# A decoder layer on one core: the inputs centred by ScalarE in place of the weights, the bias row spread by PE, loads split and reordered, new engine orders

## The reference

```python
x = x + attn(layernorm(x), Wqkv, bqkv, Wo, bo)      # 16 heads of 8, softmax over 64 positions
x = x + xattn(layernorm(x), ctx, ctx, wq, wk, wv, wo)   # autocorrelation: FFT along each row of 64, top 4 lags
x = x + ffn(layernorm(x), gate_w, w_up, w_down, expert_bias)

def layernorm(x): return (x - mean(x)) / sqrt(var(x) + 1e-5)     # no gain, no bias

def ffn(x, ...):                                     # 8 experts of 256 hidden units
    scores = sigmoid(x @ gate_w.T)
    sel = top_k(scores + expert_bias, 2)
    for e in range(8):
        w_t = sum(where(sel == e, scores[sel], 0))
        h = square(relu((x * w_t) @ w_up[e].T))
        out += h @ w_down[e].T
```

## Time and profile before

| | |
|---|---|
| median of 3 runs | 128.04 us (127.9 to 128.95) |
| time of the profiled execution | 128.05 us |
| its span | 126.3 us |
| PE busy | 112.8 us (89%) |
| DVE busy | 86.4 us (68%) |
| ACT busy | 76.6 us (61%) |
| POOL busy | 45.7 us (36%) |
| mean granted TensorE clock | 0.986 |

### The profile page before, as it was taken

One profiled execution on the slowest core, in us unless ns is written; L12 is line 12 of the kernel. 1 busy time (PEld: TensorE's weight loads), 2 busy tenths in 40 slices (PEclk: granted clock), 3 DMA queues, 4 the chain that ended last, 5 costly groups with the idle time before them and its releaser, 6 DMA issues.

```text
span 126.3 us, 4128 instructions
## 1 busy us (share of the span) xinstructions
PE 112.8 (89%) x1588; PEld 100.1 (79%) x1588; DVE 86.4 (68%) x332; ACT 76.6 (61%) x175; POOL 45.7 (36%) x81
## 2 busy tenths in 40 slices
PE   0269999979998798699999999999999999999990
PEld 0035777769875667578999999999999999999990
DVE  0224999977999457999649598927878736750671
ACT  0510549777957176937899542987914967477840
POOL 8714429525509503495633015401520040510000
PEclk9999999999999769999999999999999999999999
DMA  4899800000000000000000000100001000010001
GB/s 94 240 341 381 340 5 0 0 8 5 0 8 5 5 0 0 5 3 0 5 0 0 3 5 0 47 0 0 3 5 44 0 0 5 0 42 0 0 5 42
DMA packets 4531, 5.20 MB, mean 41 GB/s; under 512 B 288, under 2 KB 3744, under 8 KB 4384
## 3 DMA queue, kind: packets, MB, share of 16 engines
q1 hardware_dynamic: 3792, 3.87, 9.3%
q10 hardware_dynamic: 720, 1.07, 3.1%
HBM read 4.41 MB, written 0.52 MB: 39 GB/s over the span
## 4 chain that ended last, share of the span: by engine, by line
PE 83%; DVE 6%; DMA 4%; issue 3%; ACT 1%; SPq 0%; DVEq 0%
PE ps L807 23%; PE ps L796 19%; PE ps L660 6%; PE ps L689 5%; PE ps L699 5%; DMA wa_sb<-w_cen 4%; PE ps L756 3%; PE ps L646 3%; PE ps L715 2%; PE ps L670 2%; PE ps L747 1%; PE ps L639 1%; PE ps L765 1%; PE ps L739 1%; PE ps L679 1%
## 5 line engine op out<-in xcount | busy, mean ns | idle before, releaser
L807 PE MATMUL ps<-wdn_sb,hid 128*128 128x128 f32 x256 | 31.6, 276 | 0.0
L612 DVE SCALAR_TENSOR_TENSOR x<-ps,w,x 128x128 f32<-128x128 f32 x64 | 19.1, 343 | 16.7 <-PE ps L807 16.5
L807 PEld LDWEIGHTS ps<-wdn_sb,hid 128*128 128x128 f32 x256 | 29.9, 192 | 0.2
L433 ACT ACTIVATE hid<-rel 128x512 f32<-128x512 f32 x32 | 19.6, 629 | 5.9 <-PE ps L807 5.7
L427 ACT ACTIVATE rel<-ps 128x512 f32<-128x512 f32 x32 | 17.8, 595 | 7.2 <-PE ps L796 6.8
L298 POOL TENSOR_TENSOR praw<-praw,negm 128x512 f32<-128x512 f32 x16 | 16.6, 1056 | 13.4 <-DVE negm L502 13.4
L796 PE MATMUL ps<-xhi,whi 128*128 128x256 f32 x64 | 18.5, 289 | 0.0
L796 PE MATMUL ps<-xhi,wlo 128*128 128x256 f32 x64 | 18.0, 282 | 0.0
L796 PE MATMUL ps<-xlo,whi 128*128 128x256 f32 x64 | 18.0, 281 | 0.0
L286 POOL TENSOR_SCALAR rstd<-mv 128x2 f32<-128x2 f32 x12 | 2.6, 218 | 34.4 <-DVE mv L466 34.3
L796 PEld LDWEIGHTS ps<-xhi,whi 128*128 128x128 f32 x64 | 12.0, 188 | 0.4 <-POOL xlo L319 0.2
(11 more groups left out here) (102 smaller groups left out, 195.6 us busy)
## 6 DMA issues: line engine op xcount, KB each, us to landing
wup_sb<-w_up SPq DMA_DIRECT2D x2, 512.0 KB, 7.5
wdn_sb<-w_down SPq DMA_DIRECT2D x1, 1024.0 KB, 9.7
x_sb<-x SPq DMA_DIRECT2D x4, 128.0 KB, 7.0
c_sb<-ctxt SPq DMA_DIRECT2D x1, 512.0 KB, 8.4
out<-x SPq DMA_DIRECT2D x4, 128.0 KB, 1.8
con<-consts ACTq DMA_DIRECT2D x1, 328.0 KB, 5.9
row_sb<-rows ACTq DMA_DIRECT2D x1, 260.0 KB, 5.2
wmid_sb<-w_mid ACTq DMA_DIRECT2D x1, 256.0 KB, 6.7
```

The source lines that it names most:

```text
L433: nc.scalar.activation(hid[:, u % 3, :], rel[:, u % 3, :], ACT.Square).then_inc(done["sq"], 1)
L612: nc.vector.scalar_tensor_tensor(x12[:, 2 * a + t, :], psum("down", a, e)[:, D * t:D * (t + 1)], w2[:, a, t, e:e + 1], x12[:, 2 * a + t, : ...
L807: last = mm(y_ps[:, D * t:D * (t + 1)], hid[:, u % 3, 2 * P * half + P * t:2 * P * half + P * (t + 1)], wdn_sb[:, e, half, :], start=(half ...
```

## The change

The mean is now taken off the rows. `xc` and `x3c` (ACT) compute mean - x with the mean as a bias and a scale of -1, before the transposes `xt` and `xt3`, which read the new buffers. All that follows has the other sign, which is set right where results are used: `nat` and `x1` subtract, the bias row is subtracted, `eg` uses rstd in place of its negative (so POOL's `nrstd` falls away), `rel` has a scale of -1. Steps `wu`, `wc` of the qkv and gate weights and the first `wce` are gone; a `wc` of 128 columns for the query weights stays. `whi` (ACT) and `wlo` (now POOL) read the up weights from SBUF.

The bias row arrives on one partition; `rb` (PE), a product of a row of ones with it, spreads it over 128 partitions, and `rbe` (ACT) copies it. The expert bias has a small load of its own. The context is loaded by chunk, the constants and the middle weights in parts, and x in chunk 1 through ACT. All four orders are rewritten.

```diff
-C_ID, C_CEN, C_POW = 0, 128, 256
+C_ID, C_POW = 0, 128
...
-xt.0.0@0 wc.0.0@1 qkv.0.0@2 qkv.0.1@3 xt.1.0@4 wc.1.0@5 cdft.0.0@6 qkv.1.0@7 qkv.1.1@0 xt.2.0@1 cdft.1.0@2 qkv.2.0@4
+rb.0.0@0 xt.0.0@1 qkv.0.0@2 qkv.0.1@3 wc.0.0@4 xt.1.0@5 cdft.0.0@6 qkv.1.0@7 qkv.1.1@1 cproj.0.0@0 xt.2.0@2 xt.3.0@4
...
-zero.0.0 rs1.0.0 rs1.1.0 xb.0.0 rs1.2.0 psub.0.0 psub.0.1 psub.0.2 psub.0.3 rs1.3.0 psub.1.0 psub.1.1 psub.1.2 psub.1.3
+zero.0.0 zv.0.0 rs1.0.0 rs1.1.0 rs1.2.0 xb.0.0 rs1.3.0 wlo.0.0 wlo.0.1 psub.0.0 psub.0.1 psub.0.2 psub.0.3 wlo.0.2 psub.1.0
...
             sp.dma_start(wa_sb[:, 0:A_Q], w_cen[:, 0:A_Q]).then_inc(ld_qkv, 16)
-            sp.dma_start(x_sb[:, 2:4, :], xv[:, 2:4, :]).then_inc(ld_x[1], 16)
-            sp.dma_start(c_sb[:], cv).then_inc(ld_c, 16)
-            sp.dma_start(x_sb[:, 4:6, :], xv[:, 4:6, :]).then_inc(ld_x[2], 16)
-            sp.dma_start(x_sb[:, 6:8, :], xv[:, 6:8, :]).then_inc(ld_x[3], 16)
+            x_chunk(2)
+            c_chunk(0)
+            c_chunk(1)
+            x_chunk(3)
+            c_chunk(2)
+            c_chunk(3)
...
+                if name == "wlo":
+                    two = slice(2 * part, 2 * part + 2)
+                    pool.wait_ge(done["whi"], NTH[("whi", 0, part)])
+                    nc.gpsimd.tensor_tensor(wlo[:, two].rearrange("p e h -> p (e h)"), wup_sb[:, two].rearrange("p e h -> p (e h)"),
+                                            whi[:, two].rearrange("p e h -> p (e h)").bitcast(F32), ALU.subtract).then_inc(done["wlo"], 1)
...
-            act.dma_start(row_sb[:], rows.partition_broadcast(P)).then_inc(ld_row, 16)
-            act.dma_start(con[:, C_FWD:C_LEN], consts[:, C_FWD:C_LEN]).then_inc(ld_con, 16)
+            act.dma_start(x_sb[:, 2:4, :], x.rearrange("(t p) d -> p t d", p=P)[:, 2:4, :]).then_inc(ld_x[1], 16)
+            act.dma_start(row1[:], rows.unsqueeze(0)).then_inc(ld_row, 16)
+            act.dma_start(con[:, C_FWD:C_INV], consts[:, C_FWD:C_INV]).then_inc(ld_fwd, 16)
+            act.dma_start(wmid_sb[:, 0:W_O2], w_mid[:, 0:W_O2]).then_inc(ld_mid, 16)
             act.dma_start(wa_sb[:, A_Q:A_LEN], w_cen[:, A_Q:A_LEN]).then_inc(ld_wa, 16)
-            act.dma_start(wmid_sb[:], w_mid).then_inc(ld_mid, 16)
+            act.dma_start(wmid_sb[:, W_O2:W_LEN], w_mid[:, W_O2:W_LEN]).then_inc(ld_o, 16)
+            act.dma_start(con[:, C_INV:C_LEN], consts[:, C_INV:C_LEN]).then_inc(ld_con, 16)
+            act.dma_start(eb_sb[:], ebias.partition_broadcast(P)).then_inc(ld_eb, 16)
...
+                if name == "xc":
+                    act.wait_ge(done["st1"], NTH[("st1", a, 0)])
+                    if a >= 2:
+                        act.wait_ge(full["xt"], NTH[("xt", a - 2, 0)])
+                    for t in range(2):
+                        last = nc.scalar.activation(xc[:, a % 2, t, :], x_sb[:, 2 * a + t, :], ACT.Identity, bias=mv[:, a, t, 0:1],
+                                                    scale=-1.0)
+                    last.then_inc(done["xc"], 1)
...
-                if name == "wlo":
-                    dve.wait_ge(done["whi"], NTH[("whi", 0, part)])
...
+                if name == "rb":
+                    pe.wait_ge(ld_row, 16)
+                    mm(bank(name, 0), row1[:, R_ONE:R_LEN], row1[:, 0:R_ONE], start=True, stop=True).then_inc(full[name], 1)
```

203 lines of the change are left out of this document (106 added, 97 removed).

## The result

In 20 runs of each kernel on one chip the median went from 127.81 to **127.69 us** (125.79 to 129.50); the forecast was 124.0. The ratio is 0.9888, with a 95% interval of 0.9854 to 0.9922: faster by 1.1%, where 3.2% had been forecast. By the medians of all runs the gain is 0.1%. The profiled execution took 126.66 us with a span of 123.0, and its clock was whole (mean granted clock 0.998).

A forecast was written before the change was run, and what follows sets the result against it. PE and DVE were each close to being the bound up to 59.9 us, then PE ran without a gap. 128.05 - 0.8 (start) - 3.44 (`wu`) + 0.2 (chunk 2) = 124.0 us, own bounds 123.3 to 125.0, range 120.3 to 126.6.

The forecast's parts named there:

- The start: Up to `qkv.0`: it starts at 8.2 instead of 8.95 over ACT's path; 0.8 us gained, bounds 1.5 gained, 2.5 lost.
- the gain of 0.8 survives: Front, after `qkv.0`: ACT is tight, yet `qkv.1` starts at about 12.3 instead of 13.2, keeping the start's 0.8 us.
- The same pace had been priced only as a bound: First PE products: `qkv.0` stays at its slow pace; the pace rising earlier is the bound of 1.5 us gained.
- The four `wu` products: PE, centring of the up weights: four 128x512 products go, 3.44 us, all on the chain.
- PE's sum, 57.8: First `up`: by PE's work, 59.89 - 0.8 - 3.44 + 2.2 = 57.8 us, the start time chosen.
- DVE's 58.5: First `up`: with DVE's idle time as before, 59.89 - 0.8 - 2.05 + 1.5 = 58.5 us.
- the slow stretch of before: PE, 42.5 to 46.5 us: mostly at 1.2 GHz instead of 2.4, costing 1.7 us, 3.05 with the gap.
- DVE's chain decides: Rival, chance 0.15: DVE sets the first `up`, `x2.0` standing behind `pvt.3` and `val.3`; 125.7 us.
- The 1.0 us that it had for waiting on chunk 3's softmax: Before `x2.0`: DVE waits about 1 us for chunk 3's softmax if POOL is a step behind; part of a 0.15 rival.
- D: Experiments' theory, up to the first `up`: DVE's queue decides its start, so time off PE isn't on the path.
- the gap and the slow clock don't come back: Rival, chance 0.27: PE's 1.35 us gap and the slow clock's 1.7 us vanish with the new order; 121.0 us.
- The experts' stretch: From the first `up`: PE's 63.5 us loses 2.2 us moved ahead and stays gapless; 0.2 us added for chunk 2.

The follow-up runs named there:

- e1: Kernel before without the four products that centre the up weights, centring of the experts' input left out: median 127.71 us, ratio 0.9971.
- e12: Kernel after with the four up-weight centring products put back on PE, results not read: median 127.12 us, ratio 0.9911.
- a0: Kernel after, unaltered, measured a second time: median 127.57 us, ratio 0.9838 to the kernel before.
- e6: e2 with chunk 3's four `psub` on POOL replaced by a one-column memset: median 123.65 us, ratio 0.9636 to the kernel before.
- e10: e11 with DVE's `top.0` and `hit.0` moved clear of `psub`: median 124.30 us, ratio 0.9597 to the kernel before.
- e4: Kernel after with the four `wlo` steps back on DVE: median 129.09 us, ratio 1.0121 to the kernel before.
- e13: e10 with the four up-weight centring products put back on PE, results not read: median 128.04 us, ratio 1.0004 to the kernel before.
- e3: Kernel after with ACT's last three loads issued by SP behind the up weights: median 124.73 us, ratio 0.9712 to the kernel before.
- e2: Kernel after with PE's `pv.1` moved behind three steps, away from `score.3`: median 126.30 us, ratio 0.9782 to the kernel before.
- e5: e2 with 26 unread transposes of the unit matrix put where PE waits: median 125.28 us, ratio 0.9774 to the kernel before.
- e8: Kernel after with `pv.1` and `dft.0` ahead of `score.3` on PE: median 125.06 us, ratio 0.9758 to the kernel before.
- e11: Kernel after with e2's order and e3's loads together: median 124.55 us, ratio 0.9705 to the kernel before.
- e9: e1 with `wlo` moved to POOL, in the old orders: median 127.51 us, ratio 0.9957 to the kernel before.

## Why the prediction was wrong

**The start** was forecast rightly up to `qkv.0`. The table load began at 5.09 (5.0 forecast), `xc.0` and `xt.0` took 0.69 and 0.66, `qkv.0` began at 8.44 (8.2). Its gain of 0.8 us measured 0.5. But "the gain of 0.8 survives" failed: `qkv.1` came at 13.45, not 12.3, and in the chain before it had come at 13.20. The slow pace of the first products lasted until about 13.3, as it had until 13 before, so none of the start's gain was left at `qkv.1`. The same pace had been priced only as a bound. The prediction calls it PE's clock; the windows give a granted clock of 1.00 there in both kernels, so the pace is measured and its cause isn't.

**The four `wu` products** are the step that failed. The sum took "3.44 us, all on the chain" off the time in full. The chain of waits had named them rightly, but the same chain ran over DVE from 48.45 to 57.0, between the last of them and the first `up`, where the prediction read PE "nearly everywhere". The earlier trace rows had shown PE 3.9 us and DVE 6.5 us short of full over 46.7 us, so a gain of 3.44 on PE had to come out of DVE's waits. The median without them in the kernel before is that of before (e1, ratio 0.9971), and the median with them back is that of the changed kernel (e12, 0.9911). In both comparisons the kernel with less work on PE spent more time at half clock, and only a part of the 3.44 us showed at equal clock or at the first up, 1.07 in e1's profile (with 1.6 us more on DVE) and 0.9 to 2.2 in e12. The text said that "taking work off one alone buys little" and then chose PE's sum, 57.8, over DVE's 58.5 for the first up. It came at 59.04, 1.24 us later, and this in an execution without a slow stretch. The forecast had kept the slow stretch of before in its sum; with one, in a0, the first up came at 60.49, 2.7 us late, and later than before the change (59.89).

**DVE's chain decides**, a rival with 0.15, is nearest to what happened, by another route and not in full. The 1.0 us that it had for waiting on chunk 3's softmax was not seen as such; `x2.0` runs right behind `val.3` at 54.80. Beyond that stand three long steps beside `psub`, 1.90 us together, of which e6 shows 1.4 to 1.75 and e10 1.2 us to be on the path. The prediction had read the two lengths of `val` in the earlier trace rows and quoted the rule for it, from the Trainium skill, page "SBUF — State Buffer", section "Who interferes with whom": a DVE instruction with two inputs in SBUF and a GpSimd instruction that reads SBUF shut each other out. It dismissed it because most of DVE's long instructions have one input. The rule holds in this trace: `dif` and `hit` have two, and take 0.86 and 1.15 us beside `psub` where they take 0.17 and 0.29 alone. It is the short instructions with two inputs that pay, and the order should have been looked through for them. What speaks against D alone: 3.4 us more on DVE cost 1.5 us (e4), 3.44 us more on PE reached the first up with 0.86 (e12) and 2.3 (e13), and the front with 1.16 (e3). Both engines are close to being the bound, as the prediction's first paragraph has it.

**The slow clock.** The rival "the gap and the slow clock don't come back" priced the slow stretch at 1.7 us. In the kernel before, runs without it are shorter by -0.05, 0.5, 0.15 and 1.1 us in the four sets, though in the profile the chain runs over PE through the slow stretch and DVE waits 2.88 us for it. No execution of this kernel with a whole clock was profiled, and why it gains so little stays open. In the kernel after the stretch costs 1.15 to 1.7, and a second one, which the prediction named only as a thing that would make it wrong, 2.25 more in 9 of 20 runs. From the forecast's span (124.0 - 1.75 = 122.25) the profiled run's 123.0 is 0.75 more, the first up's 1.24 less 0.4 for a shorter experts' stretch (61.1 for 61.5) and rounding. That this is small is luck, since the profiled run had no slow stretch and the forecast had one. One stretch makes it 124.15, two 126.40. With some 2.1 us around the span that is 126.3 and 128.5, and the median of 127.69 lies between the two groups.

**What makes the clock fall** is settled in part. Orders with the break of 1.5 us in `pv.1` (after, a0, e3, e4) have a whole clock in 3 of 50 runs; those without it (e2, e5, e6, e8, e10, e11) in 26 of 38, and e12, where it is 0.20, in 7 of 12. The profiles say more. They hold eleven slow stretches, and each begins during a standstill of PE of 0.5 to 1.8 us or at most 1.1 us behind its end: the break of 1.35 to 1.8 us (before, a0, e1, e3, e4), one of 1.13 (e9), waits for ACT and DVE of 1.26 and 0.71 (e13, e4's second), and in e8, e10 and e11 an earlier break of 0.5 to 1.0 us in `score.2`, near 30 us. A standstill isn't enough: the profiled run of after has the break and a whole clock, and e2, e5, e6 and e12 have the earlier one, 0.75 to 1.03 us, and a whole clock too. Such standstills are common between 28 and 55 us, some five in the profile of after. So a standstill came before or with every fall, and why it is followed by one in some executions only stays open. Less work for PE went with more time at half clock in e1 and e9 against before and in after against e12; but e13, with more work than e10, had a whole clock in none of 12 runs where e10 had 3 of 6, so this is no rule.

**The break itself** falls at the same number of PE instructions in both kernels, 715 products and 716 weight loads: the window of after to 37.80 above, and of before to 40.50:

```profile
0.00:40.50 40.50, 33.16 (x715) 24.76 (x716) 28.75 (x70) 22.79 (x50) 21.12 (x29) 1.00 0.35 111
```

Everything but that count differs there: the step, the time, the neighbours. In the profiles of a0, e3, e4 and e8 the break is at 715 and 716 as well, in those of e1 and e12 one product further. It is gone where PE waits for something else just before it (e2) and small where large products run ahead of the short ones (e12). The Trainium skill, page "Runtime: NRT & Kernel Launch", section "Instruction fetch mechanics", has the crossing from one block of instructions to the next mostly hidden. Here it was not hidden in runs of very short products, if this is that crossing; that a count sets the place of the break is shown, what it counts towards isn't named in the records. The prediction used that rule only to describe its rival, which had 0.27, and was right that the break would come back.

**The experts' stretch**, 61.1 us without a gap against 61.5, `wlo` at 1.28 us on POOL within the range given, and the busy times of ACT and POOL (80.9 and 50.0 against 81 and 49) came as forecast. DVE's 85.8 is 1.8 above the 84 forecast, about what the three long steps add.

## What to carry to other kernels

Where two engines share a stretch, here 92% and 86% busy, a removal on one comes off the time only as far as the other's waits shrink with it; work out the other's sum with its waits first, and follow the chain of waits through the whole stretch. The same 3.44 us were worth nothing in the medians of two kernels and 3.7 us in that of a third, and the granted clock made most of that difference; so compare runs with the same number of slow stretches before naming an engine. After a reordering, look at which short VectorE instructions with two SBUF inputs now stand beside a long GpSimd one. And read the granted clock of every run, not of the profiled one alone: the profile of the kernel after (clock 0.998) was 1 run of 20.
